# Moving one key block to GpSimd and three pieces of order on VectorE and TensorE in a fused decoder block

## What is computed

```
x = x + linear_attention(layernorm(x))          # part A: 16 heads of 8, RoPE, phi = elu + 1, causal
x = x + softmax_attention(layernorm(x), ctx)    # part B: cross attention, 16 heads, mask over keys
x = x + moe(layernorm(x))                       # part C routes: layernorm, gate, top 2 of 8 experts
                                                # then a shared SwiGLU and the routed experts' SwiGLU
```

## Time and profile before

| | |
|---|---|
| median of 3 runs | 850.02 us (849.31 to 851.45) |
| the profiled execution | 848.82 us, its span 847.0 us |
| mean granted TensorE clock | 0.96 of full |
| busy: TensorE, its weight loads, VectorE, ScalarE, GpSimd | 732.4, 587.4, 612.4, 569.3, 542.3 us |
| the steps with attention | about 20 to 560 us of the span |
| routed experts | about 600 us to the end |

### The profile page before, as it was taken

One profiled execution on the slowest core, in us unless ns is written; L12 is line 12 of the kernel. 1 busy time (PEld: TensorE's weight loads), 2 busy tenths in 40 slices (PEclk: granted clock), 3 DMA queues, 4 the chain that ended last, 5 costly groups with the idle time before them and its releaser, 6 DMA issues.

```text
span 847.0 us, 36307 instructions
## 1 busy us (share of the span) xinstructions
PE 732.4 (86%) x14362; PEld 587.4 (69%) x14362; DVE 612.4 (72%) x1523; ACT 569.3 (67%) x1109; POOL 542.3 (64%) x697
## 2 busy tenths in 40 slices
PE   4778989889888988988998776798899999999993
PEld 3556666667656766766775555687779999997882
DVE  2247777888877878887978878559557777788773
ACT  4466899869868879878987564542336666665651
POOL 6366357458758868778887685647606666665563
PEclk9799999999989999999999988989999999999997
DMA  8321022112202202202220201500123333367673
GB/s 226 92 53 46 10 53 54 36 33 70 72 21 64 72 25 72 69 23 72 70 74 25 74 24 39 165 29 17 33 61 91 90 89 96 92 203 224 179 200 122
DMA packets 78147, 66.90 MB, mean 79 GB/s; under 512 B 8975, under 2 KB 68248, under 8 KB 77984
## 3 DMA queue, kind: packets, MB, share of 16 engines
q1 hardware_dynamic: 68512, 47.14, 21.6%
q0 software_dynamic: 8416, 16.93, 6.1%
q10 hardware_dynamic: 1056, 0.52, 0.2%
HBM read 42.46 MB, written 22.56 MB: 77 GB/s over the span
## 4 chain that ended last, share of the span: by engine, by line
PE 59%; DVE 19%; ACT 11%; issue 7%; POOL 2%; DMA 1%; SPq 0%; POOLq 0%; ACTq 0%; DVEq 0%
PE pair_x L933 11%; PE bank L951 7%; PE pair_x L727 5%; PE pair_x L637 5%; PE bank L551 4%; PE bank L744 4%; ACT Am L1039 3%; PE pair_x L809 3%; DVE mx L1585 2%; PE pair_y L809 2%; PE bank L821 2%; DVE Ex L1589 2%; PE bank L673 2%; PE bank L941 2%; PE pair_y L941 2%
## 5 line engine op out<-in xcount | busy, mean ns | idle before, releaser
L1480 POOL DMA_INDIRECT mixed<-f_y,f_x x135 | 131.2, 972 | 97.6 <-issue 65.7
L1362 POOL DMA_INDIRECT routed<-c_row,c_idx x128 | 130.5, 1020 | 75.7 <-PE bank L744 35.6
L951 PEld LDWEIGHTS bank<-Qblk,Am 128*128 128x128 f32 x540 | 79.4, 190 | 19.9 <-issue 9.1
L1221 ACT ACTIVATE qk<-pair_x 128x256 f32<-128x256 f32 x135 | 52.0, 385 | 59.4 <-PE pair_x L933 59.4
L951 PE MATMUL bank<-Qblk,Am 128*128 x540 | 83.1, 276 | 3.6 <-DVE Am L1917 2.4
L1039 ACT ACTIVATE Am<-pair_x 128x1024 f32<-128x1024 f32 x64 | 65.1, 1018 | 26.6 <-PE pair_x L637 26.6
L1074 ACT COPY ExT<-pair_x 128x1024 f32<-128x1024 f32 x64 | 64.5, 1008 | 27.1 <-PE pair_x L727 26.8
L1585 DVE TENSOR_REDUCE mx<-pair_y 128x16 f32<-128x1024 f32 x64 | 77.0, 1203 | 5.2 <-PE pair_y L637 5.1
L1589 DVE TENSOR_TENSOR Ex<-pair_y,mx 128x1024 f32<-128x1024 f32 x64 | 78.4, 1224 | 2.2
L727 PE MATMUL pair_x<-con,Ex 128*128 128x128 f32 x512 | 70.7, 283 | 10.1 <-ACT Am L1039 7.8
L637 PE MATMUL pair_y<-Kblk,KQ 32*64 32x256 f32 x1024 | 76.9, 410 | 1.0 <-issue 1.0
(11 more groups left out here) (211 smaller groups left out, 1969.8 us busy)
## 6 DMA issues: line engine op xcount, KB each, us to landing
f_x<-routed SPq DMA_DIRECT2D x135, 65.0 KB, 2.0
ctxD<-in_ctx SPq DMA_DIRECT2D x32, 256.0 KB, 4.8
ctxP<-in_ctx SPq DMA_DIRECT2D x16, 256.0 KB, 3.2
maskB<-in_mask_BxS_if SPq DMA_DIRECT2D x16, 256.0 KB, 5.2
Cblk<-mixed SPq DMA_DIRECT2D x8, 512.0 KB
Kblk<-mixed SPq DMA_DIRECT2D x8, 512.0 KB, 3.9
block_out<-X SPq DMA_DIRECT2D x14, 256.0 KB
mixed<-f_y,f_x POOLq DMA_INDIRECT x135, 3.0
```

The source lines that it names most:

```text
L951: ins = pe.matmul(banks[F_O[n % 2]][:, 0:D], f_hT[:, u % 3, c * P:(c + 1) * P], wdn[:, bass.ds(e, 1), c, :].rearrange("p o d -> p (o d)"), ...
L1362: pool.indirect_dma_start(routed[:, :], bass.IndirectOffsetOnAxis(ap=c_idx[:, d % ROW_SLOTS, t, n:n + 1], axis=0), c_row[:, d % ROW_SLOTS, ...
L1480: pool.indirect_dma_start(mixed[:, :], bass.IndirectOffsetOnAxis(ap=f_x[:, u, D + 1:D + 2].bitcast(I32), axis=0), f_y[:, u, :], None, boun ...
```

## The change

Four edits, none of which changes what is computed:

1. Block 0 of `Qblk` is made by GpSimd (`a_block(f, 0)`), between `b_c_rsqrt` and `c_scatter(first, 0)`. VectorE's `a_first_block` is gone, and the semaphore `a_qb0` with it.
2. On VectorE `c_second(d)` moves from behind `b_shift(b, 1)` to between `b_shift(b, 0)` and `b_divide(c, 1)`.
3. On VectorE `a_statistics(s + 3)` moves from before `b_shift(b, 3)` to behind `c_softmax(c)`.
4. On TensorE `b_values(b, 0)` moves behind `a_k_T(f)` and `c_norm_T(c)`.

```diff
             def a_mask_first(a, j):
-                if j == 0:
-                    pe.wait_ge(S["a_qb0"], a + 1)
-                else:
-                    pe.wait_ge(S["a_qb"], (NP - 1) * a + j)
+                pe.wait_ge(S["a_qb"], NP * a + j + 1)
...
                     c_positions(d, h)
-                if on(b):
-                    b_values(b, 0, par)
                 if on(f):
                     a_k_T(f, h, d)
                 shared(s, 4)
                 if on(c):
                     c_norm_T(c, h, odd)
+                if on(b):
+                    b_values(b, 0, par)
                 if on(b):
                     b_probs_T(b, 1, a, 2)
...
             def a_block(g, j, par):
-                if j == 1:
+                if j == 0:
                     pool.wait_ge(S["a_ph"], 2 * g + 1)
...
                     split_shared_weights()
+                if on(f):
+                    a_block(f, 0, odd)
                 if sent == PAIRED - 2:
...
                 if since(f, 2):
-                    dve.wait_ge(S["a_qb"], (NP - 1) * (f - 1))
+                    dve.wait_ge(S["a_qb"], NP * (f - 1))
...
-            def a_first_block(f, par):
-
-                dve.wait_ge(S["a_ph"], 2 * f + 1)
-                if since(f, 1):
-                    dve.wait_ge(S["a_s"], NP * (f - 1) + 1)
-                both = qT[:, par, 0:2 * T].rearrange("p (s r n) -> p s r n", s=2, r=1)
-                rows = row.rearrange("p (s r o) -> p s r o", s=1, o=1).to_broadcast([P, 2, RH, T])
-                dve.tensor_tensor(Qblk[:, 0, :, :, :], both.to_broadcast([P, 2, RH, T]), rows, ALU.mult)\
-                    .then_inc(S["a_qb0"], 1)
...
                     s_low(shared_of(s, 2) + 1)
+                if not s_is_last(s) and on(d) and batch_of(d):
+                    c_second(d)
                 if on(c):
                     b_divide(c, 1)
...
                     s_hidden(shared_of(s, 2))
-                if not s_is_last(s) and on(d) and batch_of(d):
-                    c_second(d)
...
                     a_feature(f, odd)
-                    a_first_block(f, odd)
-                if on(s + 3) and (not s_before(s, -2)):
-                    a_statistics(s + 3)
...
                     c_softmax(c)
+                if on(s + 3) and (not s_before(s, -2)):
+                    a_statistics(s + 3)
```

More of the change, by code:

```diff
@@ L343, in decoder_block @@
             a_st a_ag ac_pw ac_rsd a_xnd a_xnT_ps a_xnTd a_qk_ps a_qkd a_v_ps a_vd a_r2 a_r1 a_mn a_ex a_ph
-            a_qT_ps a_kT_ps a_qb a_qb0 a_s a_am a_av a_rc a_yd a_yT_ps a_yTd a_o a_x1
+            a_qT_ps a_kT_ps a_qb a_s a_am a_av a_rc a_yd a_yT_ps a_yTd a_o a_x1
             b_st b_ag b_mn bc_pw b_rsd b_xnd b_qT_ps b_qcd b_in b_cT_ps b_cTd b_bi b_kb b_cb b_s b_mx b_sb
```

## The result

The changed kernel takes 838.01 us, median of 5 executions (837.28 to 845.99), beside 850.02 us (849.02 to 853.1) of the kernel before on the same chip: ratio 0.9885, 95% interval 0.9841 to 0.9930. It is faster, and within the range. A ratio with its interval is an estimate of its own and need not equal the quotient of the two medians; here that quotient is 0.9859. The first comparison gives 9.8 us by the ratio (6.0 to 13.5 by its interval) and 12.0 by the medians. So the forecast of 14 us was somewhat too large against the first comparison and about twice too large against the longer ones.

What follows compares the result with a forecast made beforehand. VectorE was taken to bound odd step ends, elsewhere TensorE itself with ScalarE and GpSimd close behind. Terms 6.1 + 0.7 + 1.5 + 2.6 + 2.5 - 1.0 + 3.5 = 15.9 us, less 1.9: gain 14.0, 836.0 us, range 827 to 847.

Steps and rivals of the forecast that it cites:

- Step ends: TensorE's waits for VectorE's last shift at step ends fall to a 0.41 us floor: 6.1 us gained.
- Block 0 on GpSimd: Block ready 0.35 us earlier in two places where TensorE waits for it: 0.7 us gained (bounds 0 and 1.4).
- The sign of being wrong that the prediction gave for this edit: VectorE operations with two SBUF inputs stretched by the new block on GpSimd; no size given.
- The second choice: Six VectorE operations go into idle time; step 15's wait for the choice vanishes: 1.5 us gained (bounds 0.8 and 2.3).
- Keys and rows ahead of B's values: On TensorE, step 5's wait for positions shrinks, 2.6 us; stalls inside `b_values` fall, 2.5 us (bounds 0 and 7).
- What waits behind it: GpSimd's later scatter delays rsqrt and ScalarE's norm: 0.5 us lost in steps 9 and 13, -1.0 us (bounds 0 and -2).
- the prediction's sign of being wrong: ScalarE's norm waiting for GpSimd's rsqrt in each step; no size given.
- rival A: GpSimd becomes the bound, scatter late in even steps too: +10.5 us over ten steps, +2.8 net, 853 us; chance 0.07.
- The clock: TensorE's clock stays up after the waits in steps 5, 7 and 9: 1.6 + 1.3 + 0.6, 3.5 us gained (bounds 0 and 4.2).
- B: Most is taken back, ScalarE and GpSimd being nearly as full as VectorE: gain 7.0 us, 843 us; chance 0.20.
- C: Stalls in `b_values` go entirely (7 instead of 2.5), nothing taken back: gain 20, 830 us; chance 0.15.
- D: Change does nothing: stalls reappear as bare position waits in seven odd steps, clock falls elsewhere; 848 to 850 us; chance 0.08.

Runs made afterwards that it cites:

- the longer ones: Two later comparisons of the unedited changed kernel with the kernel before, 12 executions each: ratios 0.9930 and 0.9934, medians 840.48 and 841.78 us.
- a1: Edit 1 alone (block 0 by GpSimd) on the kernel before: ratio 0.9938 to the kernel before, median 844.48 us.
- f1: Edits 1, 2 and 3 without edit 4, on the same chip as f0: ratio 0.9859 to the kernel before, median 835.01 us.
- f0: The changed kernel with all four edits, run again beside f1, f2 and f3: ratio 0.9934 to the kernel before, median 841.78 us.
- a4: Edit 4 alone (B's first values behind key and row transposes) on the kernel before: ratio 1.0075, median 853.09 us.
- a0: The changed kernel unedited, run again for a second profile: ratio 0.9930 to the kernel before, median 840.48 us.
- a2: Edit 2 alone (second choice in VectorE's idle time) on the kernel before: ratio 0.9905, median 839.51 us.
- f2: Edits 1 and 2 alone on the kernel before: ratio 0.9868 to the kernel before, median 837.03 us.
- f3: f1 with the routing's weights moved behind the gate's softmax in odd steps up to 15: ratio 0.9856 to the kernel before, median 839.89 us.
- a3: Edit 3 alone (early statistics behind the gate's softmax) on the kernel before, slower chip: ratio 1.0019, median 909.83 us.
- b1: Edits 2, 3 and 4 with block 0 left on VectorE, slower chip: ratio 1.0013 to the kernel before, median 910.08 us.
- c1: Edits 1, 2 and 3, with edit 4 only in steps without routing, slower chip: ratio 0.9933 to the kernel before, median 901.23 us.
- b4: Edits 1, 2 and 3 without edit 4, slower chip: ratio 0.9847 to the kernel before, median 896.51 us.

## Why the prediction was right, and where it was not

*The number.* 838.01 us lies in the range, and so do the medians of the longer comparisons; but the range allowed gains of 3 to 23 us, and that is why it held. The terms did not add up to what was measured: the sum had 15.9 us, and edits 1, 2, 3 and 4 alone give 5.3, 8.1, nothing and -6 by their ratios, some 7 in all, which is what the whole change brings in the longer comparisons. A hit with a failed term in the sum is in part luck.

*Step ends, 6.1 us: right in mechanism.* The four ends that waited above the floor now wait 0.40 us or less. (Beside these four the list has six such waits, where the prediction counts seven others.) The part that did it is edit 1 (a1: 7.8 us less waiting for `Ex`); edit 3, which the prediction counted in, measures as nothing, alone and beside the others. In a1 the statistics still stand before `b_shift(b, 3)`, and waits of 0.89 and 0.96 us are left at the ends of steps 7 and 9: 1.0 us above the floor is the most edit 3 could give there. Part of the 6.1 came back inside the odd steps, as the waits of 0.80 to 0.87 us in steps 7, 9, 11 and 13, like that at 223.56.

*Block 0 on GpSimd, 0.7 us.* The start's wait fell from 5.4 to 4.3 us in total, 1.1 us, within the bounds. The block took 1.04 us, as before its neighbours did. GpSimd carries 15 us more in the span of 20 to 560 us. The sign of being wrong that the prediction gave for this edit is there as well: the first softmax operation on VectorE (line 1625, old 1636), with two inputs in SBUF, took 0.22 or 0.23 us before in steps 6, 8, 10 and 12 and now takes 1.5 to 1.8, beside a scatter and the new block. In a1, with edit 1 alone, it takes 0.2 to 0.4, so it is the edits together that stretch it.

*The second choice, 1.5 us: mis-sized.* With edit 2 alone both the waits for `c_sel` (2.3) and for the positions (5.2) went, 7.5 us, and the kernel gained 8.1. The 2.6 us of step 5 were booked under edit 4; they belong to this one, since the operations that left the way to `c_index` there were worth 4.2 us and not 1.5: the prediction priced each at 0.25 us, as undisturbed. The move was not free of GpSimd in its new place: in step 7 its last two operations took 0.69 and 0.96 us beside the rotary products.

*Keys and rows ahead of B's values, +2.6 and +2.5: the step that failed.* The bare wait for the positions came as written, 0.81 for 0.85 us, in five odd steps, and the stalls inside `b_values` fell by 8.5 us (10.5 to 2.0), more than the bound of 7. But the edit loses: +0.75% alone, 0.75% between f1 and f0, and 0.9% with the even steps alone on the slower chip. Instead of a gain (2.6 and 2.5 less the 1.0 below) it costs about 6 us.

*What waits behind it, -1.0 us: the term that was mis-sized.* The prediction named the chain (scatter, key blocks, rsqrt, ScalarE's norm) and gave it 0.5 us in two steps, since in step 9 the norm still had 0.81 us in hand. That slack belonged to a kernel in which TensorE was late for other reasons. With edits 1 and 2 VectorE's long waits at the step ends are gone, and the slack is smaller: in f1 the norm starts 0.19, 0.35, 0.49 and 0.09 us after the rsqrt in steps 7, 9, 11 and 13. With edit 4 it starts 0.09 or 0.10 us after it in all of steps 6 to 13 but one, even steps included (f0, 0.36 in step 8), and so it does without edits 1 and 2 (a4, 0.42 in step 12), where the scatter waits 2.67 us. ScalarE's norm at the end of step 7, f0 and then f1, where its rsqrt ended at 235.27 and 231.64:

```profile
235.36 1.65 ACT L983 ACTIVATE b_xn<-X,b_nm,bc_rs 128x128 f32<-128x128 f32 x4 [0.84 <-POOL b_nm L1302]
```

```profile
231.83 1.64 ACT L983 ACTIVATE b_xn<-X,b_nm,bc_rs 128x128 f32<-128x128 f32 x4
```

So the prediction's sign of being wrong, the norm waiting for the rsqrt in each step, is there. The table has, for f1 and f0 on the same chip, the length of a step from `qT` to `qT` and the time from its first `qT` to the end of the rsqrt:

| step | f1 length, rsqrt | f0 length, rsqrt | f0's scatter waits |
|---|---|---|---|
| 7 | 31.05, 31.09 | 32.32, 33.26 | 1.33 |
| 9 | 29.56, 29.60 | 31.77, 32.71 | 1.35 |
| 11 | 31.39, 32.14 | 32.36, 33.29 | 1.35 |
| 13 | 31.97, 32.02 | 32.36, 33.73 | 1.78 |
| 6, 8, 10, 12, 14 | 137.00 in all | 135.97 in all | 0.73 or 0.74 in 6 to 12, 1.11 in 14 |

In the four odd steps f0 is 4.84 us longer and its scatters wait 5.81 us for the values; in step 5, before any rows are scattered, it is 0.79 longer, the bare wait. The even steps give 1.03 back. The sum is 4.6 us. It can't be set beside the 6.8 us between the medians, since each column is one execution and the two are 11.7 us apart (841.19 and 829.53); some 7 of these lie outside steps 5 to 14. What carries over is the sign in the odd steps. Steps 7, 9, 11 and 13 together take 126.2 to 128.8 us in the four profiles with edit 4 on the faster chips (after, a0, f0, a4) and 121.8 to 124.0 in the six without (before, a1, a2, f1, f2, f3); on the slower chip a3, without edit 4, is as long as b1 with it. The mechanism is rival A's, which the prediction put at 0.07 and priced at 10.5 us over ten steps: the norm is bound by GpSimd in even steps too, but the length grows in the odd ones, by 4.8 us here.

*The clock, 3.5 us: right at the places it names, not shown for the whole.* 8.53 us at a granted clock of 0.75 became 6.72 at 1.00, 1.8 us for the 1.6 forecast. The stretch of 5.47 us in step 5 is 4.97 with the 0.7 of `b_values` now in it, 1.2 us for the 1.3. In this profile and in f0's nothing falls between 80 and 468 us; in a0's and f1's one stretch does (near 354 and 321 us). Elsewhere it was partly given back: after 468 us the clock is 0.80, 0.85 in a0 and f0, against 0.87 before. The wait of 1.89 us for `a_y` and the fall of the clock at 468.6 stand side by side, but f0 has a wait of 1.55 us at the same place and no fall before 492 us.

*Rivals.* B (843) had the right idea, that the other engines take part of it back, and its gain of 7.0 us is nearer to the longer comparisons (7.5 and 6.9 by the medians, 5.9 and 5.6 by the ratios) than the forecast's 14; it went by the busy time of ScalarE and GpSimd, and what took the gain back was edit 4, by the traces through the order of GpSimd's queue and a wait in it. C is refuted: the stalls fell by 8.5 us, more than its 7, and the gain was far from 20. That f1 has all the stalls and is the fastest says that they lie in the shadow of something else. D is refuted, for the change as a whole; on the slower chip, without edit 1, its outcome is what happened.

*What stays open.* That edit 4 costs is shown three times. That it costs by way of the scatter's wait is read from the traces and is argued, not shown; in f0's odd steps it is of the right size (5.8 us of waits, 4.8 of length). No kernel moved `c_scatter(sent, 7)` behind the key blocks with edit 4 in place, which would separate it from the bare wait for the positions, and none from the longer hold of VectorE (47.6 against 39.8 us). c1 speaks against the bare wait as the whole cause: it has none, since its odd steps keep the old order, and still loses. There the norm starts 0.09 us after the rsqrt in steps 6, 10 and 12, the even steps with edit 4, and 0.4 to 0.8 us after it in the odd ones, and yet it is the odd ones that are longer; so the path from the one to the other isn't shown. Nor is it settled why that chip is slower: there TensorE waits 24.3 us for ScalarE's `Am` in b4, against 10.0 in f1.

## What to carry to other kernels

When work is moved later in one engine's order, follow who consumes it on an engine with its own full queue, and measure that engine's slack in the kernel as it will be after the other edits, not as it was. Stalls that nothing releases may be time in which another engine catches up: in a4 7.5 us of them vanished and the kernel got slower. Price an operation as it runs at its place, with what other engines do beside it: six operations of 0.25 us, and the one behind them, stood in the way for 4.2 us. Measure edits one by one: three of these four together beat all four by 0.75%.

## What the runs showed of the hardware

VectorE operations with two inputs in SBUF took far longer while GpSimd worked on SBUF. A product of 8 columns took 2.71 us at 230.64 in the changed kernel (0.21 us at 228.96 in f1), and ended 0.03 us after the second of two key blocks that had both started after it. In f1 a product of 128 columns took 2.70 us and ended 0.16 us after the second block. The Trainium skill (SBUF — State Buffer, Who interferes with whom) says that a VectorE instruction with two SBUF inputs contends with a GpSimd instruction that reads SBUF. The trace agrees. The Trainium skill also says, in the same section, that the order of issue decides who blocks, and, where it speaks of the two-port modes of VectorE, that the first keeps the shared pair for the whole instruction. The trace doesn't show that the first goes ahead: VectorE's had started before both blocks, while the scatter ran, and got no turn between the two.

The same kernel before took 848 to 850 us in three comparisons and 908 us on the chip of the second group. A stretch at 1.2 GHz that was 10.2 us long in one profiled execution of the changed kernel and 3.4 us in another goes with a step of 28.0 us against 24.8.
